# A Perceiver block on one Trainium2 core: zeros multiplied before the first weights, parameter loads moved to ScalarE's queue, x loaded sooner

## What is computed

```python
x = x + xattn(layernorm(x), ctx, top_k=32, Wq, bq, Wk, bk, Wv, bv, Wo, bo)
#   q = LN(x) @ Wq.T + bq ; k = ctx @ Wk.T + bk ; v = ctx @ Wv.T + bv
#   softmax over the 32 largest of q.k/sqrt(512), times v, @ Wo.T + bo
x = x + wave(layernorm(x), Wqkvg, freq, damp, phase, coupling, Wout, bout)
#   kernels[h,t] = exp(-softplus(damp[h])*t) * cos(freq[h]*t + phase[h]), divided by sum |.|
#   convolved over the positions, mixed over the heads with softmax(coupling), gated
x = x + ffn(layernorm(x))      # gelu(x @ ternary(W1).T + b1) @ ternary(W2).T + b2
```

## Time and profile before

| | before |
|---|---|
| median of 3 runs | 457.74 us |
| lowest and highest of them | 457.64 and 459.82 us |
| the profiled execution: device time | 461.32 us |
| the profiled execution: span from first to last instruction | 459.5 us |
| TensorE busy | 439.7 us, 96% of the span |
| VectorE, ScalarE, GpSimd busy | 65%, 47%, 28% |
| mean granted clock of TensorE | 0.993 |

### The profile page before, as it was taken

How to read it: one execution, slowest core, us unless ns; L and a number is a source line. 1 busy time by engine, 2 the same in 40 slices (tenths; PEclk the granted TensorE clock), 3 DMA queues, 4 the chain that set the end, 5 groups by cost and what they waited for, 6 DMA issues and landing times.

```text
span 459.5 us, 5828 instructions
## 1 busy us (share of the span) xinstructions
PE 439.7 (96%) x2045; PEld 325.5 (71%) x2045; DVE 299.3 (65%) x591; ACT 215.7 (47%) x321; POOL 127.2 (28%) x195
## 2 busy tenths in 40 slices
PE   6999999799999999898999999999999999999996
PEld 2587766356567656576888888887788888888884
DVE  3898787688999999968997443646862333522224
ACT  1797764354566454384877446434542111111111
POOL 3501013032222330200003272324236643333330
PEclk9999999799999999999999999999999999999999
DMA  6999924044224314103951700000000000200002
GB/s 207 412 391 386 366 98 180 2 183 183 74 112 183 139 45 184 35 11 141 396 198 38 168 1 23 1 0 1 1 1 1 1 0 1 86 7 0 1 0 92
DMA packets 26845, 49.98 MB, mean 109 GB/s; under 512 B 6208, under 2 KB 6208, under 8 KB 25792
## 3 DMA queue, kind: packets, MB, share of 16 engines
q1 hardware_dynamic: 26816, 49.61, 30.2%
HBM read 47.49 MB, written 2.11 MB: 108 GB/s over the span
## 4 chain that ended last, share of the span: by engine, by line
PE 71%; DVE 13%; ACT 6%; DMA 5%; issue 3%; SPq 1%; POOL 0%; DVEq 0%; ACTq 0%
PE bank L1237 8%; PE bank L1239 8%; PE bank L1238 8%; PE bank L1447 7%; PE bank L1678 7%; PE bank L1676 6%; PE bank L1662 6%; PE bank L1663 6%; PE bank L1418 5%; PE bank L1344 3%; DMA wab<-w1T 2%; PE bank L1244 2%; DVE mt_lo L1026 2%; PE bank L1432 2%; DVE work L1039 2%
## 5 line engine op out<-in xcount | busy, mean ns | idle before, releaser
L792 ACT ACTIVATE g<-bank,b1c 128x512 f32<-128x512 f32 x32 | 22.0, 688 | 92.0 <-PE bank L1678 92.0
L1217 DVE CAST g_hi<-g 128x512 fp32r<-128x512 f32 x32 | 13.9, 436 | 74.7 <-ACT g L792 74.6
L594 ACT ACTIVATE mt_hi<-bank 128x512 fp32r<-128x512 f32 x64 | 38.0, 600 | 49.4 <-PE bank L1418 49.4
L1026 DVE TENSOR_TENSOR mt_lo<-bank,mt_hi 128x512 fp32r<-128x512 f32 x64 | 43.1, 684 | 18.1 <-ACT mt_hi L594 17.9
L1676 PE MATMUL bank<-xt_lo,w1s 128*128 128x512 f32 x128 | 50.8, 397 | 0.0
L1678 PE MATMUL bank<-xt_hi,w1s 128*128 128x512 f32 x128 | 50.7, 396 | 0.0
L1662 PE MATMUL bank<-w2s,g_lo 128*128 128x512 f32 x128 | 50.3, 393 | 0.2 <-DVE g_lo L1219 0.2
L1663 PE MATMUL bank<-w2s,g_hi 128*128 128x512 f32 x128 | 50.0, 390 | 0.0
L487 POOL TENSOR_SCALAR w2s<-w2t 128x512 fp32r<-128x512 int8 x32 | 19.8, 620 | 65.9 <-PE bank L1663 65.9
L445 POOL TENSOR_SCALAR qs<-qT 128x256 fp32r<-128x256 f32 x16 | 6.5, 405 | 112.8 <-PE bank L1433 93.5
L1432 PE MATMUL bank<-mt_lo,qs 128*128 128x512 f32 x64 | 30.6, 479 | 0.3 <-DVE mt_lo L1026 0.3
(11 more groups left out here) (244 smaller groups left out, 1101.0 us busy)
## 6 DMA issues: line engine op xcount, KB each, us to landing
ctxr<-ctx SPq DMA_DIRECT2D x8, 1024.0 KB, 8.5
ctx<-ctx SPq DMA_DIRECT2D x8, 1024.0 KB, 7.7
wab<-w1T SPq DMA_DIRECT2D x4, 1024.0 KB, 11.4
wab<-w2T SPq DMA_DIRECT2D x4, 1024.0 KB, 8.5
wgraw<-wgT SPq DMA_DIRECT2D x4, 1024.0 KB, 6.5
wst<-w1T SPq DMA_DIRECT2D x4, 1024.0 KB, 6.2
wst<-w2T SPq DMA_DIRECT2D x4, 1024.0 KB, 6.6
resid<-x SPq DMA_DIRECT2D x4, 512.0 KB, 6.8
```

The source lines that it names most:

```text
L594: act.activation(mt_hi[:, g % 4, :], ctx_bank(g)[:, :], ACT.Copy).then_inc(mt_hi_ok, 1)
L1026: dve.tensor_tensor(mt_lo[:, g % 4, :], ctx_bank(g)[:, :], f(mt_hi[:, g % 4, :]), ALU.subtract).then_inc(mt_lo_ok, 1)
```

## The change

Four things are altered, all in the opening. One buffer's semaphore count moves with them (`consts` counts to 5 in place of 4).

1. GpSimd first fills `mix_hi` (128 x 128, otherwise unused until the wave part) with zeros. TensorE waits for that alone and multiplies these zeros with themselves eight times in fp32, into bank 7, before step 0 of M1.
2. The four parameter loads leave SP's queue. ScalarE starts them, behind a wait for the first two weight loads (`wqk_in[0]`), as the first thing that it does.
3. SP's order becomes: weights 0, the bias columns, weights 1, x 0, weights 2, x 1, weights 3, x 2, x 3. Before, each weight pair was followed by the x load of the same number.
4. VectorE's two uses of the parameters move behind the statistics of tile 7, ScalarE's two exponentials behind `xn` of tile 7. GpSimd's two (`targ`) stay where they are, ahead of the first `rstd`.

```diff
-            def first_loads(o):
+            def first_weights(o):
                 sp.dma_start(wqraw[:, o, :], rows(wq)[:, o, :]).then_inc(wqk_in[o], 16)
                 sp.dma_start(wkraw[:, o, :], rows(wk)[:, o, :]).then_inc(wqk_in[o], 16)
-                if o == 0:
-                    sp.dma_start(cols[:, :, :], small[0]).then_inc(small_in, 16)
-                    for n, a in enumerate((freq, damp, phase)):
-                        sp.dma_start(wpar[:, n, :], a.partition_broadcast(P)).then_inc(par_in, 16)
-                    sp.dma_start(cpl[0:H, :], coup).then_inc(par_in, 16)
+            def x_load(o):
                 sp.dma_start(resid[:, 2 * o:2 * o + 2, :], x_v[:, 2 * o:2 * o + 2, :]).then_inc(x_in[o], 16)
...
-            for o in range(DC):
-                first_loads(o)
+            first_weights(0)
+            sp.dma_start(cols[:, :, :], small[0]).then_inc(small_in, 16)
+            for o in range(1, DC):
+                first_weights(o)
+                x_load(o - 1)
+            x_load(DC - 1)
...
+            pool.memset(f(mix_hi[:, :]), 0.0).then_inc(consts, 1)
             link(pool.memset(ident[:, :], 0.0))
...
         def _(act):
+            act.wait_ge(wqk_in[0], 32)
+            for n, a in enumerate((freq, damp, phase)):
+                act.dma_start(wpar[:, n, :], a.partition_broadcast(P)).then_inc(par_in, 16)
+            act.dma_start(cpl[0:H, :], coup).then_inc(par_in, 16)
...
+            first_tiles((0, 1, 2, 3, 4, 5))
+            first_xt((0, 1, 2, 3))
+            first_tiles((6, 7))
             act.wait_ge(sp_u, 1)
             act.activation(wtmp[:, 1, :], wtmp[:, 0, :], ACT.Exp, scale=-1.0).then_inc(sp_u, 1)
             act.wait_ge(cmax_ok, 1)
             act.activation(cpl[0:H, :], cpl[0:H, :], ACT.Exp, bias=nmax[0:H, :], scale=1.0,
                            accum_out=rsum[0:H, :]).then_inc(cexp_ok, 1)
...
-            first_tiles((0, 1, 2, 3, 4, 5))
-            first_xt((0, 1, 2, 3))
-            first_tiles((6, 7))
             for e in range(DC):
                 m1_hi_part(e)
...
+            for o in range(DC):
+                sumk_part(o)
+                first_stats((2 * o, 2 * o + 1))
             dve.wait_ge(par_in, 64)
             dve.tensor_reduce(nmax[0:H, :], cpl[0:H, :], AX.X, ALU.max, negate=True).then_inc(cmax_ok, 1)
             absolute(d, wpar[:, 1, :]).then_inc(sp_u, 1)
-            for o in range(DC):
-                sumk_part(o)
-                first_stats((2 * o, 2 * o + 1))
...
+            pe.wait_ge(consts, 1)
+            for n in range(8):
+                pe.matmul(bank[7][:, 0:P], f(mix_hi[:, :]), f(mix_hi[:, :]), start=True, stop=True)
             for o in range(DC - 1):
                 m1_step(o)
-            pe.wait_ge(consts, 4)
+            pe.wait_ge(consts, 5)
```

More of the change, by code:

```diff
@@ L395, in _ @@
             pool.memset(ones[:, :], 1.0).then_inc(consts, 1)
-            pool.wait_ge(consts, 4)
+            pool.wait_ge(consts, 5)
             pool.memset(lag_none[:, :], 0.0).then_inc(tpos_ok, 1)
@@ L514, in xt_part @@
                                ACT.Copy).then_inc(xt_hi_ok, 1)
[L517 to L521, removed]
             def m1_hi_part(e):
@@ L547, in _ @@
             first_tiles((6, 7))
+            act.wait_ge(sp_u, 1)
+            act.activation(wtmp[:, 1, :], wtmp[:, 0, :], ACT.Exp, scale=-1.0).then_inc(sp_u, 1)
+            act.wait_ge(cmax_ok, 1)
+            act.activation(cpl[0:H, :], cpl[0:H, :], ACT.Exp, bias=nmax[0:H, :], scale=1.0,
+                           accum_out=rsum[0:H, :]).then_inc(cexp_ok, 1)
             for e in range(DC):
@@ L570, in _ @@
             act.wait_ge(arg_ok, 1)
-            act.wait_ge(consts, 4)
+            act.wait_ge(consts, 5)
             act.activation(targ[:, :, :], targ[:, :, :], ACT.Sin, bias=half_pi[:, :], scale=-1.0).then_inc(cos_ok, 1)
@@ L906, in _ @@
                             cpl[0:H, :].unsqueeze(2).to_broadcast([H, H, E8])).then_inc(cpr_ok, 1)
-            dve.wait_ge(consts, 4)
+            dve.wait_ge(consts, 5)
             dve.tensor_reduce(mask8[:, :], ident[:, :].rearrange("p (h e) -> p e h", e=E8), AX.X,
```

## The result

| | median | lowest to highest |
|---|---|---|
| before, 9 runs | 458.04 us | 457.51 to 459.82 |
| changed, 9 runs | 461.48 us | 460.15 to 465.0 |

The ratio is 1.0076, 95% interval [1.0048, 1.0105]: 3.4 us slower, where 0.7 us faster was forecast. The time lies outside the range and has the other sign. The profiled execution of the changed kernel took 461.48 us with a span of 459.5 us, the same span as the one shown of before.

A forecast was written before the change was run, and what follows sets the result against it. TensorE's order and the chain through ScalarE bound it nearly equally. `q_product(0)` at the later of 22.9 (zeros) and 23.75 us (parameters at 9.9 plus 13.85), against 24.47: 457.74 - 0.7 = 457.0 us, range 454.7 to 459.2.

The forecast's parts named there:

- What bounds the kernel: Opening up to `q_product(0)`: TensorE's order and the chain through ScalarE nearly equal, 0.9 us of slack between them.
- The zeros: TensorE before M1: clock rises at 6.6 us, M1's 24 records end at 15.85 instead of 17.43, TensorE 1.6 us sooner.
- SP's queue: Bulk loads at some 390 GB/s: x 0 lands near 7.0 us, at worst 8.0, against 8.93; statistics 0.9 to 1.9 sooner.
- The parameters: ScalarE's four loads: the last starts at 5.8 us and takes 4.1 us to land, at 9.9; GpSimd's norms wait for it.
- L: Time at which the last of the four parameter loads has landed: 9.9 us chosen, between 8.5 and 12.3.
- the upper bound of 12.3: Latest landing of the last parameter load, in us, with 6.5 us to land as for a load among bulk loads.
- the starts are free: ScalarE starting the four parameter loads 0.47 us apart costs nothing, since it has nothing to do before 9 us.
- From L to `q_product(0)`: GpSimd's `targ` and norms, then ScalarE's work up to the first `m1_lo`: 13.85 us after L, so 23.75 us.
- the two slower powers of 0.99 us: GpSimd's norms: two of six tiles meet a `sum_k` on VectorE, their power taking 0.99 instead of 0.55 us.
- Behind `q_product(0)`: TensorE works without a wait to 52 us and its feeders have slack, so the 0.7 us gained reaches the end.
- The parameters come late: Rival at GpSimd's wait at `targ`: bulk slows ScalarE's loads, up to 1.7 us lost, 457.7 to 459.4 us; chance 0.15.
- The later slow stretch moves: Rival at TensorE's low clock after 85.7 us: up to 2.65 us less or 2 us more; chances 0.11 shorter, 0.04 longer.

The follow-up runs named there:

- e0: The kernel before, unchanged, profiled a second time: `q_product(0)` at 23.74 us; spans 456.1 and 458.0 us over 111 executions at clock 0.999 and more, and below.
- e11: e8 without the multiplied zeros: ratio 1.0021 to the kernel before.
- e2: The kernel before with only the fill of `mix_hi` and the eight zero products added: ratio 1.0005.
- e5: The changed kernel with the parameter loads on SP behind x 3 and every use of them behind the opening: ratio 1.0061 to the kernel before.
- e9: The kernel before with each x load behind the next weights on SP, nothing else altered: ratio 1.0016.
- e12: The changed kernel with the four parameter loads back on SP's queue behind the columns: ratio 1.0017 to the kernel before.
- e7: e5 without the multiplied zeros: ratio 1.0028 to the kernel before.
- e13: The changed kernel again, a single execution for a second profile: `q_product(0)` at 25.63 us against 26.84 in the first.
- e1: The changed kernel with `targ` and its wait for the parameters behind GpSimd's eight norms: ratio 1.0044 to the kernel before.
- e10: e1 with x 0 back ahead of weights 1 on SP, parameters still on ScalarE's queue: ratio 1.0035 to the kernel before.
- e14: e10 again, a single execution for a second profile: `q_product(0)` 1.5 us later than in the first.
- e8: The changed kernel with one queue, parameter loads on SP between x 0 and weights 1, `targ` and other uses late: ratio 1.0045 to the kernel before.

## Why the prediction was wrong, step by step

**What bounds the kernel.** That TensorE's order and the chain through x, the norms and ScalarE are nearly equal was right, and so was that a wait would take the place of the one removed. But the prediction saw TensorE's side as bound by the pace alone. Weights 1 bound it, in the shown execution as in e0: the row at 10.41 ends a wait for them, hidden in the list of TensorE's waits since the modelled lengths of the records before it reach over it. And the 0.7 us of room was measured in an execution later than e0 by just that.

**The zeros.** Right, with a spread: doubled pace from 5.27 us, not 6.6, in the shown profile, and from 5.1 to 7.0 in the other ten with zeros, against 7.8 to 10.4 without (in e11 the rise falls into a stop); M1's 24 records end at 15.4, not 15.85. M1 started 0.27 us late, as said. What wasn't named is what comes late for a faster TensorE in the order of before: weights 1 (e2, 1.32 us). By the page "TensorE: Matmul & The Clock Gate" of the Trainium skill, "Part 1: The HAM clock gate", activity releases the throttle. Products of zeros do so here, by the times just given.

**SP's queue.** The first step that failed. x 0 was issued at 3.06, as said, and was to land near 7.0, at worst 8.0; it landed near 9.8 (statistics at 9.60 to 9.88 in three profiles with this order and ScalarE's loads, at 8.8 in two). The rate was taken from the slices of the earlier trace rows behind the opening; up to 8 us it was 264 to 268, and 254 to 308 without ScalarE's loads (e5). The one megabyte ahead of x 0's end was counted, but not that it comes at two thirds of the rate. It isn't the second queue alone: with one queue and x behind weights 1 the statistics start at 9.61 and 9.62 too (e9, e12), behind the hole, and at 9.03 and 9.46 with no parameters ahead (e5, e7).

**The parameters.** The second step that failed, and here the one that decides the sum: L was 13.9 and 13.2 in the two profiles of the changed kernel, not 9.9, beyond the upper bound of 12.3. Of its two terms the time from issue to landing failed in both: coup took 6.8 and 7.5 us, where 4.1 was chosen and 6.5 was the upper bound by the earlier trace rows. The start failed in one: "the starts are free" and 0.47 us apart came from a queue with nothing beside it. In the shown profile they took 0.39, 0.79, 1.64 and 0.69 us, so the last began at 7.10 and not at 5.8; in e13 it began at 5.71. So the 4.0 us too few are 1.3 of start and 2.7 of landing in the one, and the 3.3 all of landing in the other. Between bounds of 2.7 and 6.5 I chose 4.1, a row measured in an empty stretch, though the row of a load among bulk was the nearer case.

Beside that choice stood the rule of "DMA: Bandwidth & Descriptors", "Queues, rings and completion order", in the Trainium skill, by which engines take turns between queues at packet granularity. I read it as "small loads need not wait". The changed kernel's queue table gives ScalarE's queue 464 packets for 25 KB, 29 for each of 16 engines if they share evenly. If each takes its turn behind one packet of the bulk, that is by estimate 29 waits and not one, so the rule itself doesn't promise an early landing; whether the turns are what the loads wait for wasn't tried. Behind bulk on SP's own queue the same four took 7.0 to 10.3 us (e5).

**From L to `q_product(0)`.** L + 13.85 would be 27.8. The first `m_lo` was there near 26.55: the two slower powers of 0.99 us didn't come. The six powers took 0.54 to 0.57 us each, though VectorE's `sum_k` ran beside GpSimd at 15.18 and 18.23; it met two `ln_nb` instead, which took 0.38 and 0.69. The step was 1.2 us too long, and a forecast with the right L would have come out near 461.

**Behind `q_product(0)`** nothing is given back: 2.37 us there, and 2.37 at the first score product (54.93 for 52.56). Right.

**The rivals.** "The parameters come late" was the one that came, with the mechanism it named; its price of 1.7 us stopped at the bound of L. "The later slow stretch moves" was right as a danger: the shown profile has none at 85.7 to 91 us and a fall at 19 to 22 instead, e13 has one from 88 us on. A mean clock below 0.999, that is a low stretch somewhere, comes in 57 of before's 111 executions, in seven of nine here, and in 91 of 133 of the kernels e1 to e12. Whether a changed opening makes it likelier stays open.

## What to carry to other kernels

A hole of 2 us that small scattered loads make in a transfer queue wasn't filled here by giving them a second queue: they then took two to three times as long to land as on the first queue in e0 and e12, and landings of the bulk differed by up to 1.9 us between two profiles of one kernel (e10, e14; 0.7 us between the two of before, with one queue). When a wait is moved to later data, ask who stands behind it; here eight norms did. And take a second profile of the kernel before, where the gain that is hoped for (0.7 us) is no larger than what two executions of it differ by.

## What was not expected of the hardware

- Starting a load on ScalarE's queue took 0.39 to 1.64 us beside SP's bulk, and 0.38 to 0.67 in e13; on SP four of the same lie 0.47 us apart. SP's own starts grew too once bulk was under way: up to 1.55 us in the changed kernel, and to 1.50 us in e5, where no other queue carries loads.
- Loads of 1 to 8 KB took 5.8 to 8.0 us from issue to landing beside bulk of another queue (changed, e13), 7.0 to 10.3 behind bulk of their own (e5), and 2.5 to 4.1 behind weights 0 alone (before, e0, e12).
- In e8 TensorE stood still for 2.1 us with the clock up; behind that the granted clock stood at 0.50 over 12 to 14 us. In e14 it stood still for 1.86 us up to 14.50, and the clock stayed at 1.00.
- Kernels with the zeros have 1.91 to 2.00 us outside the span in the median, those without 1.78 to 1.81; e13, a single execution with zeros, has 1.79. Where the difference comes from wasn't looked into.
